# Expert token transposes in replicated fp32, the experts' waits cut piece by piece, and one bias matmul in place of two

## The reference

```
x = x + xattn(layernorm(x), ctx, mask, Wq, bq, Wk, bk, Wv, bv, Wo, bo, gamma, beta, residual_scale)
x = x + moe(layernorm(x), gate_weight, w_gate, w_up, w_down)

# xattn: 16 heads of 64, 4 batches of 1024 tokens, width 1024; scores clipped to +-50, masked softmax
delta = layernorm(clip(residual_scale, 0, 0.3) * (ctx @ Wo.T + bo)) * gamma + beta

# moe: 64 experts, the best 8 of a token, inner width 384
scores = softmax(x @ gate_weight.T);  topk_w, topk_idx = top_k(scores, 8);  topk_w /= topk_w.sum()
g, u = ragged_dot(sorted_tokens, w_gate), ragged_dot(sorted_tokens, w_up)
out  = ragged_dot(silu(g) * u, w_down)
y    = sum over the 8 of out * topk_w
```

## Time and profile before

| | us |
|---|---|
| median of 3 runs | 6835.75 (6833.43 to 6835.9) |
| the profiled execution, whole | 6831.15 |
| its span, first to last instruction | 6829.2 |
| granted TensorE clock, mean | 0.991 of full |
| PE busy / DVE / ACT / POOL | 6695.8 / 3294.1 / 3004.1 / 1120.7 |
| output pass, first to last matmul group | 2302.7 to 2829 |
| experts pass, first token transpose to the end | 2859.4 to 6829.2 |

### The profile page before, as it was taken

How to read it: one execution, slowest core, us unless ns; L and a number is a source line. 1 busy time by engine, 2 the same in 40 slices (tenths; PEclk the granted TensorE clock), 3 DMA queues, 4 the chain that set the end, 5 groups by cost and what they waited for, 6 DMA issues and landing times.

```text
span 6829.2 us, 104167 instructions
## 1 busy us (share of the span) xinstructions
PE 6695.8 (98%) x34594; PEld 5941.0 (87%) x34595; DVE 3294.1 (48%) x4252; ACT 3004.1 (44%) x3636; POOL 1120.7 (16%) x1013
## 2 busy tenths in 40 slices
PE   9999999999999999799999999999999999999998
PEld 7888887887888777699999999999999999999998
DVE  4443325999999798632443333322422323333333
ACT  3222225888888545333444344422422333333333
POOL 1000000000000255411111111111111111111111
PEclk9999999999999999899999999999999999999999
DMA  8863555555555666465776667654644556556665
GB/s 259 228 197 144 156 138 145 130 129 126 128 128 133 181 165 169 136 154 121 189 200 166 157 163 185 162 123 105 184 105 105 136 128 164 147 139 159 159 148 149
DMA packets 692631, 1047.87 MB, mean 153 GB/s; under 512 B 259953, under 2 KB 490097, under 8 KB 692530
## 3 DMA queue, kind: packets, MB, share of 16 engines
q0 software_dynamic: 109792, 368.12, 24.8%
q1 hardware_dynamic: 426352, 381.24, 21.7%
q10 hardware_dynamic: 156386, 297.29, 12.6%
HBM read 724.14 MB, written 322.31 MB: 153 GB/s over the span
## 4 chain that ended last, share of the span: by engine, by line
PE 53%; DMA 2%; issue 1%; ACT 1%; DVE 1%; ACTq 0%; SPq 0%; POOLq 0%; DVEq 0%
PE moe_ps_gate L1332 5%; PE moe_ps_gate L1333 5%; PE moe_ps_gate L1334 5%; PE moe_ps_up L1334 5%; PE moe_ps_y L1321 5%; PE moe_ps_up L1332 5%; PE moe_ps_up L1333 5%; PE moe_ps_y L1319 5%; PE moe_ps_y L1320 5%; PE moe_ps_xT L1309 3%; DMA out<-moe_y,moe_rec_s 1%; PE moe_ps_hT L1340 1%; DMA moe_rec_s<-table 1%; ACT moe_y L1371 0%; DVE moe_gu_lo L1426 0%
## 5 line engine op out<-in xcount | busy, mean ns | idle before, releaser
L1332 PE MATMUL moe_ps_gate<-moe_gu_hi,moe_xT_hi 128*128 128x384 f32 x2288 | 793.3, 347 | 25.4 <-DVE moe_gu_lo L1426 20.9
L1436 DVE TENSOR_TENSOR moe_hidden<-moe_silu,moe_ps_up 128x384 f32<-128x384 f32 x286 | 158.5, 554 | 1305.1 <-PE moe_ps_up L1334 1016.6
L1333 PE MATMUL moe_ps_gate<-moe_gu_lo,moe_xT_hi 128*128 128x384 f32 x2288 | 768.9, 336 | 0.0
L1334 PE MATMUL moe_ps_gate<-moe_gu_hi,moe_xT_lo 128*128 128x384 f32 x2288 | 768.5, 336 | 0.0
L1334 PE MATMUL moe_ps_up<-moe_gu_hi,moe_xT_lo 128*128 128x384 f32 x2288 | 765.1, 334 | 0.0
L1332 PE MATMUL moe_ps_up<-moe_gu_hi,moe_xT_hi 128*128 128x384 f32 x2288 | 764.2, 334 | 0.0
L1333 PE MATMUL moe_ps_up<-moe_gu_lo,moe_xT_hi 128*128 128x384 f32 x2288 | 764.2, 334 | 0.0
L1371 ACT ACTIVATE moe_y<-moe_ps_y,moe_rec_s 128x1024 f32<-128x1024 f32 x287 | 320.7, 1117 | 906.5 <-PE moe_ps_y L1321 494.7
L1319 PE MATMUL moe_ps_y<-moe_d_hi,moe_hT_hi 128*128 128x512 f32 x1722 | 700.4, 407 | 1.9 <-DVE moe_hT_lo L1441 1.9
L1289 POOL DMA_INDIRECT out<-moe_y,moe_rec_s x287 | 458.6, 1598 | 1443.1 <-ACT moe_y L1371 1370.1
L1321 PE MATMUL moe_ps_y<-moe_d_hi,moe_hT_lo 128*128 128x512 f32 x1722 | 677.3, 393 | 0.0
(11 more groups left out here) (202 smaller groups left out, 14172.5 us busy)
## 6 DMA issues: line engine op xcount, KB each, us to landing
first_raw<-in_w_gate ACTq DMA_DIRECT2D x63, 1536.0 KB, 7.0
first_raw<-in_w_up ACTq DMA_DIRECT2D x63, 1536.0 KB
moe_raw_d<-in_w_down ACTq DMA_DIRECT2D x63, 1536.0 KB
proj_a_raw<-in_ctxT POOLq DMA_DIRECT2D x64, 512.0 KB, 5.0
kst<-proj_o SPq DMA_DIRECT2D x256, 128.0 KB, 2.8
vst<-proj_o SPq DMA_DIRECT2D x64, 512.0 KB, 2.6
qst<-proj_o SPq DMA_DIRECT2D x256, 128.0 KB, 2.2
att_kt<-kst SPq DMA_DIRECT2D x64, 512.0 KB, 3.6
```

The costliest lines, as they stand in the source:

```text
L1332: nc.tensor.matmul(o[:, 0:I], xT_hi[:, c], gu_hi[:, b, k, c], start=(c == 0), stop=False)
L1333: nc.tensor.matmul(o[:, 0:I], xT_hi[:, c], gu_lo[:, b, k, c], start=False, stop=False)
L1334: last = nc.tensor.matmul(o[:, 0:I], xT_lo[:, c], gu_hi[:, b, k, c], start=False, stop=(c == C - 1))
```

## The change

Three things at once.

**The bias.** `bo_rows` has 128 rows, all zero but row 0 (`bo_hi`) and row 32 (`bo_lo`); `ones_rows` is 128 x 128 ones. One matmul with 128 rows replaces two with one row. POOL clears `bo_rows` ahead of its other set-up, and ACT's copy into row 0 waits for that.

**The experts' waits and order.** ACT and DVE split all eight gate and up pieces of the next expert in a row, ahead of `output(t - 1)` and `hT_hi`. PE waits for one piece ahead of the two chunks that use it. The routing weight moves from `output` (ACT) to `hidden` (DVE, now an instruction with a per-row factor), with a record tile of its own, `rec_w`: a third 1 KB DMA per tile on SP, between the other two, behind a wait for `hidden` of the tile before. `output` becomes a plain copy and waits for the scatter of the tile before rather than for `rec_s`; that wait is now POOL's, in `add`. ACT's first two experts are written out ahead of the loop.

**The transposes.** `tokens`, the identity for them (`ident_r`, a POOL copy of `ident`) and the PSUM tile `xT` become fp32r; the gather writes through an fp32 view of the same bytes. Shapes, count and order of the eight transposes stay.

```diff
-                    nc.tensor.matmul(o[:, b, cols], ones_row[:], bo_hi[:, cols], start=False, stop=False)
-                    nc.tensor.matmul(o[:, b, cols], ones_row[:], bo_lo[:, cols], start=False, stop=True).then_inc(gemm_done, 1)
+                    nc.tensor.matmul(o[:, b, cols], ones_rows[:], bo_rows[:, cols], start=False, stop=True).then_inc(gemm_done, 1)
...
+                    sp.wait_ge(hidden_done, t + 2)
+                    sp.sem_inc(sp_passed, 1)
+                    record(rec_w, t + 1, rec_w_in)
...
-                        last = nc.tensor.transpose(xT_ps[:, c], tokens[:, c * P:(c + 1) * P], ident[:])
+                        last = nc.tensor.transpose(xT_r[:, c], tokens[:, c * P:(c + 1) * P], ident_r[:])
...
-                        if e is not None:
-                            pe.wait_ge(w_lo_done, PIECES * e + (k + 1) * (C // 2))
                         for c in range(C):
+                            if e is not None and c % 2 == 0:
+                                pe.wait_ge(w_lo_done, PIECES * e + k * (C // 2) + c // 2 + 1)
...
-                def output(t):
+                def output(t, is_first=False):
                     act.wait_ge(down_done, t + 2)
-                    act.wait_ge(rec_s_in, 16 * (t + 2))
-                    nc.scalar.activation(y[:], y_ps[:], ACT.Copy, scale=rec_s[:, 1:2]).then_inc(y_done, 1)
+                    if not is_first:
+                        act.wait_ge(added, 16 * (t + 1))
+                    nc.scalar.copy(y[:], y_ps[:]).then_inc(y_done, 1)
...
-                        split(e, b, 0, EARLY)
-                    output(t - 1)
+                        split(e, b, 0, GU)
+                    output(t - 1, is_first)
                     act.wait_ge(hT_done, t + 2)
                     nc.scalar.copy(hT_hi[:], hT_ps).then_inc(hT_hi_done, 1)
-                    if e is not None:
-                        split(e, b, EARLY, GU)
...
-                    nc.vector.tensor_tensor(hidden[:], silu[:], up_ps[:, 0:I], ALU.mult).then_inc(hidden_done, 1)
+                    dve.wait_ge(rec_w_in, 16 * (t + 1))
+                    nc.vector.scalar_tensor_tensor(out=hidden[:], in0=silu[:], scalar=rec_w[:, 1:2], in1=up_ps[:, 0:I],
+                                                   op0=ALU.mult, op1=ALU.mult).then_inc(hidden_done, 1)
```

More of the change, by code:

```diff
@@ L1291, in add @@
                         in_=y[:], in_offset=None, compute_op=ALU.add).then_inc(added, 16)
+                pool.wait_ge(ready, 1)
+                nc.gpsimd.tensor_copy(ident_r[:], ident[:]).then_inc(ready, 1)
                 gather(0)
@@ L1409, in expert @@
                     if has_next:
[L1410 removed]
+                        expert_tiles(act, e, lambda t: tile(t, e + 1, 1 - b, has_second, isinstance(e, int) and e == 0), tile)
                         split(e + 1, 1 - b, GU, PIECES)
@@ L1415, in expert @@
                         expert_tiles(act, e, tile, tile)
-                experts(act, expert)
+                experts(act, expert, peel=True)
                 last_tile = act.value_load(dir_sb[0:1, last_at:last_at + 1], min_val=E - 1, max_val=MAX_TILES - 2)
```

46 lines of the change are left out of this document (26 added, 20 removed).

## The result

The changed kernel takes 6764.16 us (median of 4 runs, 6762.57 to 6764.94) where the kernel before takes 6834.59 beside it: a ratio of 0.9899, 95% interval 0.9887 to 0.9911, 70 us less. The profiled execution takes 6763.85 us, and its span answers the earlier trace rows.

What follows compares the result with a forecast made beforehand. PE, busy 98% of the span, was taken as the bound, with DVE close behind in the output pass. Transposes 0, bias 19 and experts' waits 14 made 33 us: 6835.75 - 33 = 6803 us, range 6780 to 6826.

Steps and rivals of the forecast that it cites:

- The transposes: 0 forecast: Token transposes in the experts pass: replicated fp32 changes nothing, 0 us; bounds 119 us off and 278 us on.
- The failed step: Experts pass: from two replicated-fp32 loads 0.11 us apart, a replicated-fp32 transpose is held by its load at 0.11 us.
- Rival A: Token transposes: a replicated-fp32 load hides or is short in transpose form, 119 us more gained, 6684 us; chance 0.07.
- The bias: 19 forecast: Output pass: one bias matmul saves PE 33.4 us, but DVE becomes the bound, so 19 us are won.
- DVE's period without its wait: Output pass: time between DVE's normalisation starts less its wait for ACT's `out_d`, 15.71 - 0.56 = 15.15 us per tile.
- The bound of 12: Output pass: lower bound of the bias gain, 12 us, if DVE then waits for ACT's roots instead.
- its signs: Things to see in the new trace, among them 0.69 us from line 902's start to the transposes' after its bias.
- The experts' waits: 14 forecast: Experts pass: of 36 us that aren't PE's own work, 22 stay and 14 go; bounds 0 and 30.
- ACT's queue of about 20 us per single-tile expert: Experts with one tile: ACT's queue, against PE's 13.66 us, is the bound; the order only shifts where it bites.
- The sum: Whole kernel: transposes 0, bias 19 and experts' waits 14 make 33 us, from 6835.75 to 6803 us.
- Costed at nothing: Side costs put at 0 us: POOL's clearing (0.9 if uncovered) and `ident` copy (at worst 0.5), SP's third record, `hidden`'s factor.

Runs made afterwards that it cites:

- 64-column runs: Seven of eight token transposes load 64 columns of tokens for 128: plain fp32 in the kernel before, 6832.49 us; replicated fp32 in the changed kernel, 6722.23 us.
- the join: Bias and experts' changes together; without the format it is the changed kernel with token transposes back in plain fp32, 6804.28 us, ratio 0.9959.
- the reordered issues: Changed kernel with gate and up loads issued earlier, inside the weight pieces, and the down load issued behind the next silu: 6754.06 us, ratio 0.9884.

## Why the prediction was wrong, point by point

**The transposes: 0 forecast, 48 us of PE's work and 40 to 44 us of time found.** The failed step is the sentence "Behind the transposes stand two replicated-fp32 loads which nothing but each other holds up, and they start at 5011.91 and 5012.02, 0.11 us apart", from which followed "a replicated-fp32 transpose would be held by its load at 0.11 us, as the plain one is now". The two loads belong to matmuls, and a transpose's load is another kind, 0.14 us long and not 0.19, and in replicated fp32 0.085 us apart and not 0.11. That the plain transpose stood at nearly the same 0.109 looked like a confirmation and was a coincidence: its moving side takes as long. The 64-column runs show which side held which format. The warning stood in the trace of before: the loads of the transposes are in it with their own length of 0.14. Their least distance, 0.085, is not, since there the moving side paced them. Rival A named the right direction with the wrong size: it let the load hide altogether, 119 us, at a chance of 0.07. What happened lay between it and the forecast, at 48, and no case covered the stretch between; that is also why the range was too short.

**The bias: 19 forecast; 14.8 by the spans, 18 by the medians.** PE's price was right, 0.23 for the step, and so was the change of bound: DVE's waits for `out_d` fell from 24.6 to 4.2 us, and PE's waiting for `out_h` rose from 7.4 to 22.4. The mis-sized term is DVE's period without its wait: 15.15 us read, 15.32 measured. DVE's starts span 484.3 us before (2319.0 to 2803.3) and 469.6 after (2318.9 to 2788.5), 14.7 less. The gaps left on DVE are short, 0.4 us at most, 4.2 us in 13. The bound of 12, "if a third of the waits is merely renamed", was the nearer one by the spans. Among its signs the prediction gives 0.69 us from line 902's start to the transposes'; its own sum makes that two steps of 0.23, 0.46, and the rows have 0.47.

**The experts' waits: 14 forecast; 12.8 by the spans, 14 by the medians.** The wait for weight pieces went (20.9 to 2.6 us) and waits for `hidden` and low tokens of 1 to 3 us came in its place, where the prediction looked for them. With the plain transposes first and last hidden transpose are 3918.2 us apart, where it said 3915. The statement that "ACT's queue of about 20 us per single-tile expert against PE's 13.66 is the true bound" holds roughly in its number, 18.15 us at the place read, and not in its words: ACT isn't full. A third of the loop is standing for DVE, issuing loads and reading the table, and moving an instruction from ACT to DVE made the time worse.

**The sum.** Bias and waits together were forecast at 33 us; the join without the format measures 30 by the medians, 27 by the spans. The three parts do not quite add: faster transposes on top of the join bring 40 where they bring 44 alone. More waits in the join are not the reason. Both times PE's tile gets shorter while the loop through ACT and DVE doesn't, and waits take part of it back: about 10 us alone, about 6 in the join, where PE's waits for `hidden` rise from 8.3 us to 11.2. The difference stands in the steady tile, 13.47 us alone and 13.49 in the join, 5 us over 285 tiles. What makes it is not shown.

**Costed at nothing, and right:** POOL's clearing of `bo_rows` and its copy of `ident`, SP's third record, the factor in `hidden`. The first token transposes and the first hidden ones moved with the output pass and by no more.

**What stays open.** Of the 32 us, 10.5 go with half of the gate and up bytes, and 9.5 with the reordered issues. Whether these are the same microseconds was not tried, nor what the last 21 would take. No run takes the scatter's flight out of the tiles behind an expert's first.

## What to carry to other kernels

Before a duration or a distance is taken for another instruction, compare the length of the two records: a load that is 0.14 us long is not priced by one that is 0.19. When an operation is held by one of two sides that take nearly the same time, a row can't tell which; so the range must reach over the whole stretch between "the other side binds at once" and "nothing binds". And where an engine looks like the bound but waits for a second one in every round, moving work to that second engine can lengthen the loop, as it did here by 17 us: look at the hand-overs first. Before a run is read as the answer to a theory, look whether the wait that it was to remove is gone.

## What the runs showed of the hardware that was not expected

- A transpose of 128 x 128 costs PE 0.109 us in plain fp32 and about 0.085 in replicated fp32. The first is held by the moving side (64 loaded columns for 128 change nothing), the second by the load (with 64 it falls to about 0.06).
- The load of a transpose is 0.14 us long in either format (0.11 with 64 columns), that of a replicated-fp32 matmul 0.19.
- Behind a group of fast transposes some 0.04 us are given back: from the last transpose's start to the second matmul's behind it, 0.383 us pass where 0.342 did. A group of three gains 0.043 us in all, a group of eight 0.17.
- Going from operands of 128 rows to 64 and back cost PE about 0.2 and 0.14 us in the one run that did it, as much as its seven half-sized transposes save.
- A matmul of 512 columns with a single row costs 0.32 to 0.34 us, and so does the 128-row matmul ahead of it; one of 128 rows among its like costs 0.23. What of it is the single row and what the change of row count no run tells apart.
